# Attention and mixture of experts: scores from fp32r parts in four bands of 32 rows instead of bf16 parts in two bands of 64

## What is computed

```python
qkv = x @ W_qkv.T + b_qkv                      # x: 32 x 256 x 128
att = einsum('bthd,bshd->bhts', q, k) / sqrt(8)
att_v = einsum('bhts,bshd->bthd', softmax(att), v)
x = layernorm(x + att_v @ W_out.T + b_out)
scores = sigmoid(x @ gate_w.T)                 # top 2 of scores + expert_bias
shared = (silu(x @ sw1.T) * (x @ sw3.T)) @ sw2.T
x = layernorm(x + shared + sum over the two of score * expert(x * score))
```

## Time and profile before

| | us |
|---|---|
| median of 3 runs | 806.11 (803.26 to 808.59) |
| the profiled execution, its own time | 806.83 |
| span of the trace in it | 804.8 |

### The profile page before, as it was taken

How to read it: one execution, slowest core, us unless ns; L and a number is a source line. 1 busy time by engine, 2 the same in 40 slices (tenths; PEclk the granted TensorE clock), 3 DMA queues, 4 the chain that set the end, 5 groups by cost and what they waited for, 6 DMA issues and landing times.

```text
span 804.8 us, 18923 instructions
## 1 busy us (share of the span) xinstructions
PE 757.6 (94%) x6148; PEld 460.7 (57%) x6148; DVE 639.9 (80%) x1382; ACT 521.4 (65%) x1047; POOL 480.6 (60%) x653
## 2 busy tenths in 40 slices
PE   1699999999999999999998699999999999999996
PEld 0234555555555555555554466666666666666663
DVE  5578999999999999999997286666666666666765
ACT  1138888888888888888888265555555555555542
POOL 3446767667667677676633345555666565656654
PEclk9999999999999999999999789999999999999998
DMA  5653656656565566566520442455644444444541
GB/s 162 166 128 114 175 160 169 170 157 155 165 165 158 169 169 161 160 166 164 149 76 22 131 116 75 131 132 131 130 129 123 118 126 116 128 119 117 133 120 52
DMA packets 201534, 108.79 MB, mean 135 GB/s; under 512 B 10480, under 2 KB 201072, under 8 KB 201456
## 3 DMA queue, kind: packets, MB, share of 16 engines
q1 hardware_dynamic: 200048, 105.88, 49.5%
q10 hardware_dynamic: 1408, 1.91, 0.9%
HBM read 73.41 MB, written 33.82 MB: 133 GB/s over the span
## 4 chain that ended last, share of the span: by engine, by line
PE 87%; issue 3%; DVE 3%; POOL 3%; DMA 2%; ACT 1%; SPq 1%; POOLq 0%; DVEq 0%; ACTq 0%
PE bank L666 15%; PE bank L829 14%; PE bank L638 10%; PE bank L673 8%; PE bank L675 8%; PE bank L674 8%; PE bank L651 7%; PE bank L748 3%; PE bank L728 2%; PE bank L768 2%; PE bank L735 2%; PE bank L752 2%; PE bank L800 2%; PE bank L775 1%; DVE negmax L937 1%
## 5 line engine op out<-in xcount | busy, mean ns | idle before, releaser
L937 DVE TENSOR_REDUCE negmax<-bank 128x2 f32<-128x512 f32 x512 | 320.1, 679 | 25.3 <-PE bank L651 22.7
L515 ACT ACTIVATE probs<-bank 128x512 f32<-128x512 f32 x512 | 291.7, 605 | 61.0 <-PE bank L638 57.2
L651 PE MATMUL bank<-k_stack,q_stack 48*128 48x256 bf16 x1024 | 163.7, 283 | 9.4 <-DMA k_stack<-k_parts_dram 5.3
L673 PE MATMUL bank<-x_hi,hi_w 128*128 128x512 f32 x288 | 166.5, 578 | 1.3 <-DVE q_stack L1011 0.9
L616 ACT ACTIVATE q_stack<-k_stack 128x512 f32<-128x512 f32 x128 | 80.7, 631 | 122.7 <-DVE k_stack L1001 121.2
L638 PE MATMUL bank<-q_stack,k_stack 50*128 50x256 bf16 x1024 | 156.8, 275 | 2.9 <-ACT probs L515 2.5
L1001 DVE TENSOR_TENSOR k_stack<-bank,probs 128x512 f32<-128x512 f32 x128 | 88.2, 689 | 75.5 <-PE bank L675 69.6
L666 PE MATMUL bank<-probs,v_aug 128*32 128x256 f32 x2048 | 137.9, 387 | 0.4 <-ACT attT L526 0.4
L638 PEld LDWEIGHTS bank<-q_stack,k_stack 50*128 50x128 bf16 x1024 | 75.4, 95 | 86.7 <-ACT probs L515 44.5
L675 PE MATMUL bank<-x_lo,hi_w 128*128 128x512 f32 x288 | 115.3, 400 | 0.0
L674 PE MATMUL bank<-x_hi,lo_w 128*128 128x512 f32 x288 | 115.3, 400 | 0.0
(11 more groups left out here) (101 smaller groups left out, 1061.4 us busy)
## 6 DMA issues: line engine op xcount, KB each, us to landing
probs<-route_dram SPq DMA_DIRECT2D x128, 256.0 KB, 5.9
q_stack<-q_parts_dram SPq DMA_DIRECT2D x64, 192.0 KB, 3.3
k_stack<-k_parts_dram SPq DMA_DIRECT2D x64, 192.0 KB, 4.1
k_parts_dram<-k_parts SPq DMA_DIRECT2D x32, 192.0 KB, 2.1
q_parts_dram<-q_parts SPq DMA_DIRECT2D x32, 192.0 KB, 2.1
xT_sb<-xT SPq DMA_DIRECT2D x32, 128.0 KB, 2.2
k_parts_dram<-k_parts SPq DMA_DIRECT2D x32, 128.0 KB, 2.0
q_parts_dram<-q_parts SPq DMA_DIRECT2D x32, 128.0 KB, 2.0
```

Source lines behind the costliest of these rows:

```text
L515: nc.scalar.activation(probs[h][:], score_ps[EXP_BANK[h]][:].rearrange("p (j t) -> p j t", j=NT), ACT.Exp).then_inc(exp_done, 1)
L651: mm = pe.matmul(max_ps[MAX_BANK[h]][:, i * T:(i + 1) * T], q_stack[b.ring][first:last, h // 2, i * P:(i + 1) * P], k_stack[b.ring][first: ...
L673: pe.matmul(ps[:], w_hi[m][:, n, :], hi[:], start=start, stop=False)
L937: nc.vector.tensor_reduce(negmax[b.ring % 2][:, :, column], max_ps[MAX_BANK[h]][:].rearrange("p (i s) -> p i s", i=NT), AX_X, ALU.max, neg ...
```

## The change

Splits are now in fp32r (PARTS = 2 parts, NC = 3 products, ROWS = 24), so a head with its two rows of maxima fits in 32 partitions (BAND), and four heads lie above each other in a stack (QUADS = 4 groups). The stacks are fp32 in memory and read as fp32r. Maxima use the band two further on than the shifted scores (`h ^ 2`). Moreover the order within a block is changed (both heads for the first half of the sequence, then both for the second), `var_eps` moves from DVE to POOL, the constants and expert weights are loaded later and their split is spread over six slots, and batch 0's q is split by DVE.

```diff
-QPART = (0, 0, 0, 1, 1, 2)
-KPART = (0, 1, 2, 0, 1, 0)
+QPART = (0, 0, 1)
+KPART = (0, 1, 0)
+FOUR, BAND = 4, 32
...
-        q_stack = [sb(f"q_stack{r}", [P, PAIRS, T], BF16) for r in range(RING)]
+        q_stack = [sb(f"q_stack{r}", [P, QUADS, T]) for r in range(RING)]
...
-        q_parts, k_parts = ([sb(f"{n}{r}", [P, PARTS, T], BF16) for r in range(2)] for n in ("q_parts", "k_parts"))
-        max_rows = sb("max_rows", [2 * H, T], BF16)
+        q_parts, k_parts = ([sb(f"{n}{r}", [P, PARTS, T], F32R) for r in range(2)] for n in ("q_parts", "k_parts"))
+        max_rows = sb("max_rows", [2 * H, T])
...
 # SP
-                        for u in range(2):
-                            sp.dma_start(stack[b.ring][HALF * u:HALF * u + ROWS, :, :],
-                                         dram[b.ring].rearrange("(g u) d c t -> u (d c) g t", u=2)[u]).then_inc(stack_in[b.ring], 16)
+                        for u in range(FOUR):
+                            sp.dma_start(stack[b.ring][BAND * u:BAND * u + ROWS, :, :],
+                                         dram[b.ring].rearrange("(g u) d c t -> u (d c) g t", u=FOUR)[u]).then_inc(stack_in[b.ring], 16)
...
-                    for u in range(2):
-                        sp.dma_start(q_stack[b.ring][HALF * u + ROWS:HALF * u + ROWS + 2, :, :],
-                                     max_rows[H * u:H * u + H, :]).then_inc(max_in[b.ring], 16)
+                    for u in range(FOUR):
+                        sp.dma_start(q_stack[b.ring][BAND * u + ROWS:BAND * u + ROWS + 2, :, :],
+                                     max_rows[2 * QUADS * u:2 * QUADS * (u + 1), :]).then_inc(max_in[b.ring], 16)
...
 # GpSimd: rk, rq and the third parts are gone
-                    pool.tensor_tensor(rk[:], kf[:], k_split[:, 0, :], ALU.subtract).then_inc(split_step, 1)
...
+                    pool.wait_ge(mv_set, b.count(NT, NT))
+                    pool.tensor_scalar(var_eps[:], mv[:, :, 1], EPS, None, ALU.add).then_inc(eps_set, 1)
                     pool.wait_ge(eps_set, b.count(1, 1))
                     pool.tensor_tensor(rstd[:], var_eps[:], minus_half[:, 0:NT], ALU.pow).then_inc(rstd_set, 1)
...
+                for m in range(2):
+                    for n in range(0, NE, 3):
+                        if t.soft.c == split_slot(m, n):
+                            pool.wait_ge(w_hi_set, m * (NE // 3) + n // 3 + 1)
+                            pool.tensor_tensor(w_lo[m][:, n:n + 3, :], w_stage[m][:, n:n + 3, :], w_hi[m][:, n:n + 3, :],
+                                               ALU.subtract).then_inc(w_lo_set, 1)
...
 # ACT
-                        if b.c == 0 and not b.looped:
-                            load_constants()
...
+                if t.proj.c == 1:
+                    load_constants()
...
 # PE, row_maxima_scores
-                other = 1 - h % 2
-                first, last = HALF * other, HALF * other + ROWS
-                mm = pe.matmul(max_ps[MAX_BANK[h]][:, i * T:(i + 1) * T], q_stack[b.ring][first:last, h // 2, i * P:(i + 1) * P],
-                               k_stack[b.ring][first:last, h // 2, :], start=True, stop=True)
+                m = h ^ 2
+                first, last = BAND * (m % FOUR), BAND * (m % FOUR) + ROWS
+                mm = pe.matmul(max_ps[MAX_BANK[h]][:, i * T:(i + 1) * T],
+                               q_stack[b.ring][first:last, m // FOUR, i * P:(i + 1) * P].bitcast(F32R),
+                               k_stack[b.ring][first:last, m // FOUR, :].bitcast(F32R), start=True, stop=True)
...
 # PE, a block
                 for p in range(PAIRS):
-                    for h in (2 * p, 2 * p + 1):
-                        for n in range(NT):
+                    for n in range(NT):
+                        for h in (2 * p, 2 * p + 1):
...
 # DVE
-                        nc.vector.tensor_scalar(var_eps[:], mv[:, :, 1], EPS, None, ALU.add).then_inc(eps_set, 1)
```

186 lines of the change are left out of this document (104 added, 82 removed).

## The result

The changed kernel takes 822.06 us (817.6 to 822.64, four runs) where the kernel before takes 805.94 in the same session: a ratio of 1.019 with a 95% interval of 1.0151 to 1.0228, slower. The forecast was 791 with a range to 807: wrong in sign. Medians here are of all executions of a kernel, while ratios and intervals leave out those over 1.5% above its fastest (1 of 8 with the loads at head 6, 2 of 10 with both edits, and 1 each with late loads, short maxima, the second K projection and the last filler). The profiled execution has a span of 820.8 us against 804.8, so the 16.0 us are in it, and the question is where.

The account below looks back on a forecast made before the run. PE bounded the kernel, with DVE 0.26 us behind it in the attention slot; 9.8 us from the slots, 4 from the start and 1 from the split summed to 15, giving 791 us (786 to 798; 8 in 10: 776 to 807).

Parts of the forecast that it names:

- Block of 0.40 us, loads side by side: PE's attention blocks: four bands' fp32 loads run in parallel, block 0.40 us instead of 0.54, PE needs 11.2 us per slot.
- the serial rival: PE's blocks: fp32 loads run one after another, block 0.97 us, slot 15.8, about 910 us; chance 0.12, milder form included.
- the ring: Block 0, maxima, copy, DMAs, next block 0: 12.2 us at worst; slot taken as 11.95, 9.8 us off in 28 slots.
- The rival with this wait: PE's wait for the rows of maxima eats all the slot's gain: slot 12.25, start alone leaves 801 us; chance 0.14.
- that cover: Expert-weight load DMAs run beside stacks read one slot later; without this slack each costs up to its few us.
- The clock: Rival: PE, less filled, gets full clock later or falls back; each half-clock slot costs over 3 us, 815 with five; chance 0.05.
- The start: Pipeline start: batch 0's maxima begin 9 us earlier; net gain about 4 us, bounds 1 to 8.
- the fill: Two slots with maxima alone, PE at 1.2 GHz: DVE idling loses 4 us, two more maxima DMAs cost 1.2.
- DVE sets the pace at 11.8 to 11.9: Steady attention slot: DVE needs some 11.7 us without `var_eps`, plus 0.1 to 0.2 lost to the new block order.
- from the end of that maximum: Block order: PE yields scores 0.55 us after head 2p-2's maximum while DVE has 0.52 us of work, so DVE loses almost nothing.
- The split in six pieces: Expert-weight split: pieces of 0.4 us beside ACT's 1.7 us of slack per slot; gain 1 us, 0 to 1.5.
- The last slots: Draining slots at the attention's end, where ACT and the norm's chain decide: zero change, -1 to 1 us.

Follow-up runs that it names:

- the loads at head 6: Changed kernel with the three expert-weight loads issued at head 6 of their slots instead of head 12: 809.54 us, ratio 1.0054.
- both edits: Changed kernel with two DMAs instead of four for the rows of maxima, and expert-weight loads at head 6 instead of 12: 802.21 us, ratio 0.9951.
- late loads: Changed kernel with loads and splits of expert weights ten slots later, loads still at head 12: 825.73 us, ratio 1.0235.
- short maxima: Changed kernel with two maxima DMAs, loads at head 6, old block order, plus two of sixteen maxima over 128 keys only: 799.56 us, ratio 0.9939.
- the second K projection: Changed kernel with two maxima DMAs, loads at head 6, old block order, plus every slot's K projection done twice: 812.27 us, ratio 1.0064.
- the last filler: Changed kernel, two maxima DMAs, loads at head 6, old block order, twelve unused matmuls at start, one of 256 columns per block before slot 0: 790.89 us.
- the run with the old order: Changed kernel with two maxima DMAs and loads at head 6, plus a block's matmuls head by head again: 797.41 us, ratio 0.9881.
- the old order alone: Changed kernel with only a block's matmuls put back head by head, four maxima DMAs and loads at head 12 kept: 825.29 us, ratio 1.0237.
- the one with two DMAs: Changed kernel with its rows of maxima put in by two DMAs instead of four, loads left at head 12: 805.63 us, ratio 1.0002.

## Why the prediction was wrong

**Block of 0.40 us, loads side by side: right.** Measured 0.44, with the bands' loads together; the serial rival (0.12) is out. PE's need was put at 11.2 per slot and is some 11.4 (from the kernel with short maxima).

**The rows of maxima: the mechanism was named, the term was mis-sized, and this is the first step that failed.** The prediction had the ring: 8.1 us to the copy and 4.1 from it, "12.2 at worst", and then took 3.4 for the second part, "with the 0.42 us of a stack's DMA for an issue". The row of the very same DMA said 1.26 us for two. Measured: 8.10 and 4.29, slot 12.39. The bound was nearly met and the value chosen against the nearest row: 28 x 0.35 = 9.8 us of gain became some 2.5 of loss. The rival with this wait ("slot 12.25, 801") had 0.14.

**The loads of expert weights: the second step that failed, and the larger part of the 16 us.** "Their DMAs run beside stacks that are read one slot before they are needed": true of the stacks, but the load was issued 1.4 us behind the first of the four DMAs of maxima, which are read in the same slot by PE's very next block. The price was written down ("if that cover is gone, each costs up to its few us, at most three times") and left out of the sum and of every rival. Measured: 2 us each at PE, and with the clock 10.6 in all.

**The clock: named with 0.05, and 4.5 of the 16 us.** "815 with five such" slots is close in kind: half clock in slots 3 and 5 behind PE's gaps, 4.5 us. They are what slots 2 to 5 lost beyond the waits; no run took the clock's share by itself. The prediction treated the clock as chance; the runs show it as what a gap of 2 to 3 us can bring with it.

**The start: 9 us for the first maxima, measured 8.6; 4 and 1.2 given back in the fill, measured 3.4.** Both near enough; the 1.2 for two more DMAs is 0.8 (slot -1 takes 14.41 with four and 13.58 with two). Not foreseen are the 4.8 us in slots 0 and 1: the full clock came at 70.5 us instead of 62.2. This is not settled. Among the runs of four-band kernels without unused matmuls it came at 51.8, 54.0 and 54.2 in three, at 68.3 to 72.5 in six, and at 55 and 56 with a relapse in two, with slot 0 at 13.6 to 14.0 in the first kind and 17.2 to 18.1 in the second, and kernels with the same first slots fall on both sides. The kernel before shows 62.2, and 58.1 with epsilon by GpSimd. That the earlier start makes the late value likelier is possible and not shown. So of the start's forecast gain of 4 us some 0.3 are left (8.5 less 3.4 less 4.8), and 4.8 of the 16 us have no shown cause beyond the clock. The same scatter moves the other kernels' times by several us.

**DVE sets the pace at 11.8 to 11.9: wrong.** It never did. With the ring out of the way the slot is 12.10, and neither adding to DVE (12.20) nor taking from it (12.10) moves it by what was changed. The step that failed is "from the end of that maximum": it traced PE and DVE against each other and took ACT's 10.57 of 12.30 for slack; by the trace of short maxima the blocks that come close together find ACT still at its exponentials. So even with both waits mended the gain was 26 x 0.2 = 5 us and the start's few, not 15. **The split in six pieces** did what was said: 0.51 us each on ACT, and slots 6 to 9 with them take 12.4 like the others.

**The last slots** were put at -1 to 1 and cost 2.7. In slots 28 and 29 the ring goes on (12.4 us each, before 12.0 and 11.7), but it isn't all: with both waits mended the stretch is no shorter, at a half clock for 3.4 us of it. This stays open. **The experts** were zero, measured zero.

The mended edits show which parts hold: side-by-side bands, the earlier start, late constants. The sign was lost on two DMA placements: with both mended, the forecast would have been right in sign and still too high in size.

## What to carry to other kernels

Cost a wait with the issue time of the very DMA in question, and where a ring's bound stands above the slot, treat it as the forecast until a row says otherwise. Before a large load is moved into a running pipeline, list what else is issued around it and who reads it first. All ten loads here that were issued between 0.2 us ahead of the first small DMA and 0.5 us ahead of the last cost PE some 2 us or more, and mostly the clock; the same load 3.3 us ahead of the first, or (with two small DMAs) 0.8 us behind the start of the last, was free. An engine that is busy 86% of a slot is not slack: look at what it does between the two moments at which the bottleneck meets it.

## What was not expected of the hardware

A pair of matmuls in other bands passes one whose band is taken. In the run with the old order the queue holds head 2p's two halves and then head 2p+1's; both heads' first halves start within 0.02 us and head 2p's second half 0.21 us later; which is which can be told, since only second halves raise a semaphore, and none of the first four does. The Trainium skill, "TensorE: Matmul & The Clock Gate", section "The mechanism", says that matmuls start and end strictly in program order; the trace of that run differs, and the measurement decides. "TensorEngine Tiling (Array Packing)", section "Key Properties", says that tiles load and multiply in parallel; by that rule, the trace agrees, for fp32 weights of 24 and 26 rows too (four loads of 0.18 us within 0.01).

An issue of these SBUF to SBUF DMAs takes SP 0.61 us and they follow 0.65 apart, where those of a stack follow 0.42 apart; with rows of four bands in one DMA (a partition step of 32) it takes 0.54 and they follow 0.58 apart (1.12 for two), and ACT's queue issues at 0.62 at the same time as SP's.

A gap of PE of 2.0 to 2.8 us in a busy slot went with a fall to half clock in ten of eleven cases: two of three in the changed kernel, all three with the old order alone, the one with two DMAs, and all four with late loads, these at 141 to 261 us. The fall came between 0.2 us before the gap's end and 1.7 us behind it and lasted 3.4 to 10.2 us. The traces with the loads at head 6 have no gap over 1.5 us between slot 0 and 400 us and, once the full clock had settled (by 73 us in all), no fall there. But two executions with both edits and one with the loads at head 6 had a mean granted clock of 0.955 to 0.959, where the others of these kernels had 0.982 to 0.994. No trace of them was kept, so a fall without such a gap is not ruled out.
